# A transformer block with routed experts on one core: full-height bias planes, expert numbers read earlier, joins moved

## The reference

```python
# x: 2 x 1024 x 256, float32; 16 heads of 128 in 4 groups; 8 experts, 2 per token
mod = silu(c) @ wmod                      # sa, ca, ga, sb, cb, gb for each batch
h = layernorm(x) * (1 + ca) + sa
x = x + ga * attention(h, wq, bq, wkv, bkv, wo)   # causal
h = layernorm(x) * (1 + cb) + sb
gate_logits = h @ gate_w.T
top_vals, top_idx = top_k(gate_logits, 2)
w = softmax(top_vals)
y_all = einsum('td,eod->teo', h, expert_w) + expert_b
y_sel = take_along_axis(y_all, top_idx)
x = x + gb * sum(y_sel * w)
```

## Time and profile before

| | |
|---|---|
| timed runs | median 933.34 us of 3 (931.67 to 953.36) |
| profiled execution | 924.07 us, its span 922.3 us |
| mean granted TensorE clock | 0.99 of full |
| busy: PE, VectorE, ScalarE, GpSimd | 888.7 (96%), 741.4 (80%), 544.0 (59%), 325.8 (35%) us |
| chain that ended last | PE 91%, VectorE 5%, ScalarE 2%, issue 1%, DMA 1% |
| DMA | 43.09 MB, mean 47 GB/s |

### The profile page before, as it was taken

How to read it: one execution, slowest core, us unless ns; L and a number is a source line. 1 busy time by engine, 2 the same in 40 slices (tenths; PEclk the granted TensorE clock), 3 DMA queues, 4 the chain that set the end, 5 groups by cost and what they waited for, 6 DMA issues and landing times.

```text
span 922.3 us, 16979 instructions
## 1 busy us (share of the span) xinstructions
PE 888.7 (96%) x5399; PEld 774.2 (84%) x5399; DVE 741.4 (80%) x1672; ACT 544.0 (59%) x1255; POOL 325.8 (35%) x404
## 2 busy tenths in 40 slices
PE   6999999999999999999999999999999999999895
PEld 5788888888888898888888989898988888877573
DVE  6777888888888888878888888888889898865454
ACT  4577666666666666664766666666666666635241
POOL 4464122222222222232434444444222245372815
PEclk9999999999999999999999999999999999999898
DMA  6000710000000000300000000000000003513642
GB/s 240 7 12 13 255 32 12 12 11 11 11 15 15 16 11 7 103 6 1 24 12 14 12 13 12 12 12 12 13 12 13 12 24 133 167 52 105 194 147 80
DMA packets 36651, 43.09 MB, mean 47 GB/s; under 512 B 3061, under 2 KB 33815, under 8 KB 36503
## 3 DMA queue, kind: packets, MB, share of 16 engines
q1 hardware_dynamic: 34216, 35.94, 12.0%
q0 software_dynamic: 2304, 6.29, 2.1%
q10 hardware_dynamic: 64, 0.02, 0.0%
HBM read 32.02 MB, written 15.20 MB: 51 GB/s over the span
## 4 chain that ended last, share of the span: by engine, by line
PE 91%; DVE 5%; ACT 2%; issue 1%; DMA 1%; POOL 0%; SPq 0%; DVEq 0%; ACTq 0%
PE ps_t L1048 13%; PE ps_s L937 10%; PE ps_s L941 9%; PE ps_s L938 9%; PE ps_o L929 7%; PE ps_o L933 7%; PE ps_o L930 7%; PE ps_m L937 3%; PE ps_m L941 3%; PE ps_m L938 3%; PE ps_m L929 3%; PE ps_m L933 3%; PE ps_m L930 3%; PE ps_o L1058 1%; PE ps_s L1299 1%
## 5 line engine op out<-in xcount | busy, mean ns | idle before, releaser
L1410 ACT ACTIVATE pt_hi<-ps_t 128x512 fp32r<-128x512 f32 (+2 forms) x320 | 170.9, 534 | 124.6 <-PE ps_t L1048 124.2
L1460 ACT ACTIVATE probs<-ps_s,neg_max 128x128 f32<-128x128 f32 (+7 forms) x256 | 189.9, 742 | 79.5 <-DVE neg_max L1853 76.2
L1862 DVE TENSOR_TENSOR pt_lo<-ps_t,pt_hi 128x512 fp32r<-128x512 f32 (+2 forms) x320 | 192.2, 601 | 12.9 <-ACT pt_hi L1410 9.0
L1853 DVE TENSOR_REDUCE neg_max<-ps_s 128x1 f32<-128x128 f32 (+7 forms) x256 | 192.3, 751 | 3.7
L1048 PE MATMUL ps_t<-ident,probs 128*128 128x128 f32 x1152 | 188.6, 272 | 0.9 <-DVE pt_lo L1862 0.9
L695 POOL TENSOR_TENSOR q_lo<-raw,q_hi 128x512 fp32r<-128x512 f32 x60 | 77.4, 1289 | 310.8 <-ACT q_hi L1410 310.8
L1048 PEld LDWEIGHTS ps_t<-ident,probs 128*128 128x128 f32 x1152 | 141.9, 141 | 20.7 <-DVE pt_lo L1862 4.9
L937 PE MATMUL ps_s<-k_hi,q_hi 128*128 128x512 f32 (+2 forms) x354 | 148.5, 420 | 2.4 <-ACT probs L1460 2.4
L1900 DVE SCALAR_TENSOR_TENSOR acc<-ps_m,rsum,acc 128x256 f32<-128x256 f32 x256 | 111.3, 476 | 17.6 <-PE ps_m L941 17.0
L941 PE MATMUL ps_s<-k_hi,q_lo 128*128 128x512 f32 (+2 forms) x354 | 123.4, 349 | 0.0
L938 PE MATMUL ps_s<-k_lo,q_hi 128*128 128x512 f32 (+2 forms) x354 | 122.6, 346 | 0.0
(11 more groups left out here) (300 smaller groups left out, 1728.3 us busy)
## 6 DMA issues: line engine op xcount, KB each, us to landing
slot_out_dram<-y_slot SPq DMA_DIRECT2D x38, 128.0 KB, 1.7
wq_raw<-in_L_attn_wq_dram SPq DMA_DIRECT2D x32, 128.0 KB, 2.3
wo_raw<-in_L_attn_wo_dram SPq DMA_DIRECT2D x32, 128.0 KB, 2.0
wkv_raw<-in_L_attn_wkv_dram SPq DMA_DIRECT2D x2, 1024.0 KB, 6.5
acc<-in_L_attn_x_dram SPq DMA_DIRECT2D x2, 1024.0 KB, 16.1
we_raw<-in_L_ffn_expert_w_dram SPq DMA_DIRECT2D x1, 2048.0 KB, 8.4
slot_rows<-slot_rows_dram SPq DMA_DIRECT2D x2, 1024.0 KB, 7.6
slot_rows_dram<-in_L_attn_x_dram SPq DMA_DIRECT2D x1, 1920.0 KB, 17.6
```

The costliest lines, as they stand in the source:

```text
L1410: return nc.scalar.activation(dst, src, ACT.Copy, scale=scale)
L1460: nc.scalar.activation(probs[par][:, prob_offset(i):prob_offset(i) + w], ps_s[:, i % 2, col:col + w], ACT.Exp, bias=neg_max[:, par, i:i + ...
L1853: nc.vector.tensor_reduce(neg_max[:, par, i:i + 1], ps_s[:, i % 2, col:col + w], AXIS_X, ALU.max, negate=True).then_inc(max_set, 1)
L1862: nc.vector.tensor_tensor(pt_lo[:, q % PT, lo:CH], ps_t[:, q % 2, lo:CH], pt_hi[:, q % PT, lo:CH].bitcast(F32), ALU.subtract).then_inc(pt_ ...
```

## The change

- `bias_planes` is cleared on all 128 partitions and `bias_ones` is 128 x 128; both bias matmuls contract over 128 rows, 126 of them zero. GpSimd now does the multiply and the subtraction, in two operations, and VectorE's `bias_low` is gone.
- PE loads the 23 numbers after step 1 of the last frame, and the 15 numbers after the first pair of d = 1.
- On VectorE and ScalarE the halves of near slots 23 and 24 come right behind `mix(1)`. Join 0 alone stays behind `mix(1)`; joins 1 to 5 stand at near slots 2, 4, 7, 9 and 12; joins 6 and 7 inside `mix(2)`, 8 and 9 inside `mix(3)`, 10 and 11 last.
- `finish` of d = 0, 1 and 3 goes to VectorE; GpSimd keeps d = 2, behind its last gather. The ring of gather semaphores is three long. SP's stores follow the new order.

```diff
-GATHERS = 4
+GATHERS = 3
+JOIN_AT = {2: 1, 4: 2, 7: 3, 9: 4, 12: 5}
-        bias_ones = moe("bias_ones", [FREE, P], F32R)
+        bias_ones = moe("bias_ones", [P, P], F32R)
...
+            store_mixed(0)
+            store_mixed(1)
             store_joined(0)
-            store_mixed(0)
-            store_joined(1)
-            store_mixed(1)
             for s in range(SLOTS1):
                 store_slot(s)
-                if s % 2 == 1 and s // 2 + 2 < NT:
-                    store_joined(s // 2 + 2)
-            store_joined(NT)
-            store_mixed(2)
-            for j in range(NT + 1, JOINS):
+                if s - 1 in JOIN_AT:
+                    store_joined(JOIN_AT[s - 1])
+            for j in range(NT - 2, NT + 2):
                 store_joined(j)
             store_mixed(3)
+            store_joined(NT + 2)
+            store_joined(NT + 3)
+            store_mixed(2)
...
             def bias_tables():
+                flat = bias_planes[0:FREE, :, :].rearrange("p x o -> p (x o)")
                 pool.wait_ge(t_mm, NS * (B * HEADS - 1))
                 pool.iota(bias_sign[:, :], pattern=[[0, 8]], base=0, channel_multiplier=1,
...
+                pool.memset(bias_ones[:, :].bitcast(F32), -1.0).then_inc(bias_set, 1)
+                pool.memset(bias_planes[:, :, :].bitcast(F32), 0.0).then_inc(bias_step, 1)
+                pool.wait_ge(bias_step, 2)
                 pool.wait_ge(bias_in, 16 * FREE)
+                pool.tensor_scalar(flat, bias_raw[:, :], 1.0, 1.0, ALU.mult, ALU.mult).then_inc(bias_step, 1)
+                pool.wait_ge(bias_step, 3)
+                pool.tensor_scalar(flat, flat.bitcast(F32), bias_sign[:, 0:1], 1.0, ALU.mult,
+                                   ALU.mult).then_inc(bias_step, 1)
+                pool.wait_ge(bias_step, 4)
+                pool.tensor_tensor(flat, flat.bitcast(F32), bias_raw[:, :], ALU.subtract).then_inc(bias_set, 1)
...
-            for j in range(NT):
-                gather(j)
-                if j == 2:
-                    finish(0)
-                if j == 5:
-                    finish(1)
-            for j in range(NT, JOINS):
+            for j in range(JOINS):
                 gather(j)
             finish(2)
-            finish(3)
...
+                    if very_last and q == 1:
+                        pe.wait_ge(place_set, 1)
+                        first_e.extend(chosen(slot_expert_u, SLOTS))
...
-                nc.tensor.matmul(bank, bias_ones[:, :], bias_planes[0:FREE, bass.ds(e, 1), :].rearrange("p x o -> p (x o)"),
+                nc.tensor.matmul(bank, bias_ones[:, :], bias_planes[:, bass.ds(e, 1), :].rearrange("p x o -> p (x o)"),
...
-            pe.wait_ge(place_set, 1)
-            slot_e = chosen(slot_expert_u, SLOTS)
...
                 for e2 in range(EXPERTS // 2):
                     experts(d, e2)
+                    if d == 1 and e2 == 0:
+                        pe.wait_ge(n_place_set, 1)
+                        near_e.extend(chosen(n_expert_u, SLOTS1))
...
                 mix_first(d)
                 if d + 2 < HALF:
                     hidden2_hi(d + 2)
                 if d == 1:
+                    slot_upper(SLOTS)
+                    slot_upper(SLOTS + 1)
                     weigh_first(0)
-                    weigh_first(1)
-                if d == 3:
-                    weigh_first(NT)
-                    weigh_first(NT + 1)
-            weigh_first(NT + 2)
-            weigh_first(NT + 3)
+                if d == 2:
+                    weigh_first(NT - 2)
+                    weigh_first(NT - 1)
+            for j in range(NT, JOINS):
+                weigh_first(j)
...
-                        if q == 10:
-                            bias_low()
...
                 if d == 2:
-                    slot_lower(SLOTS)
-                    slot_lower(SLOTS + 1)
                     for s in range(SLOTS, ALL_SLOTS):
                         if s + 2 < ALL_SLOTS:
                             slot_lower(s + 2)
-                        i = s - SLOTS
-                        if i % 2 == 1 and i // 2 + 2 < NT:
-                            join(i // 2 + 2)
-                mix(d)
+                        if s - SLOTS in JOIN_AT:
+                            join(JOIN_AT[s - SLOTS])
+                mix(d, {2: {3: NT - 2, 5: NT - 1}, 3: {3: NT, 5: NT + 1}}.get(d, {}))
                 if d + 2 < HALF:
                     hidden2_lo(d + 2)
                 if d == 1:
+                    slot_lower(SLOTS)
+                    slot_lower(SLOTS + 1)
+                    finish(1)
                     join(0)
-                    join(1)
-                if d == 3:
-                    join(NT)
-                    join(NT + 1)
+                elif d != 2:
+                    finish(d)
             join(NT + 2)
             join(NT + 3)
```

More of the change, by code:

```diff
@@ L468, in adaln_block @@
         coef_step, coef_set, first_mixed = sem("coef_step"), sem("coef_set"), sem("first_mixed")
-        moe_mm, mixed, ysum_set, yout_set = (
-            sem("moe_mm"), sem("mixed"), sem("ysum_set"), sem("yout_set"))
+        moe_mm, mixed = sem("moe_mm"), sem("mixed")
+        ysum_set, yout_set = [[sem(f"{name}{i}") for i in range(2)] for name in ("ysum_set", "yout_set")]
         out_done = [sem(f"out_done{i}") for i in range(2)]
@@ L1358, in experts @@
                 pair = slice(2 * e2, 2 * e2 + 2)
-                nc.tensor.matmul(bank, bias_ones[:, :], bias_planes[0:FREE, pair, :].rearrange("p x o -> p (x o)"),
+                nc.tensor.matmul(bank, bias_ones[:, :], bias_planes[:, pair, :].rearrange("p x o -> p (x o)"),
                                  start=True, stop=False)
@@ L1365, in experts @@
                 last.then_inc(moe_mm, 1)
-            def chosen(table, count):
-                return nc.values_load_multi_w_load_instructions(
-                    table[0:1, 0:count], engines=[mybir.EngineType.PE], min_val=0, max_val=EXPERTS - 1,
-                    skip_runtime_bounds_check_because="a sum of seven comparisons lies in 0 to 7")[1]
             n = B * HEADS - 1
@@ L2286, in hidden2_lo, with finish, mix @@
                                         ALU.subtract).then_inc(h2_lo_set, 1)
-            def mix(d):
+            def finish(d):
+                par = d % 2
+                if d >= 2:
+                    dve.wait_ge(out_done[par], 16 * (d // 2))
+                dve.wait_ge(mixed, (d + 1) * LATER_MIXES)
+                nc.vector.tensor_tensor(y_sum[:, par, :], y_even[:, par, :], y_odd[:, par, :], ALU.add).then_inc(ysum_set[par], 1)
+                dve.wait_ge(ysum_set[par], 2 * (d // 2) + 1)
+                nc.vector.tensor_tensor(y_sum[:, par, :], y_sum[:, par, :], row_of["gb1"], ALU.mult).then_inc(ysum_set[par], 1)
+                dve.wait_ge(ysum_set[par], 2 * (d // 2) + 2)
+                nc.vector.tensor_tensor(y_out[:, par, :], y_sum[:, par, :], acc[:, NT + HALF + d, :],
+                                        ALU.add).then_inc(yout_set[par], 1)
+            def mix(d, joins):
                 par = d % 2
@@ L2300, in mix @@
                                                    coef[:, d, e:e + 1], y, ALU.mult, ALU.add).then_inc(mixed, 1)
+                    if e in joins:
+                        join(joins[e])
             def join(j):
```

51 lines of the change are left out of this document (20 added, 31 removed).

## The result

The changed kernel takes 922.68 us (median of 4 runs, 921.62 to 924.42) beside 933.3 for the kernel before: ratio 0.9894 [0.9868, 0.9919]. That is 1.1% less, inside the 2% within which the prediction counts two kernels as the same, and 10.7 us of the 23.1 that it had worked out. The profiled execution took 923.59 us, its span is 921.6.

A forecast was written before the change was run, and what follows sets the result against it. PE, busy 96% of the span, was taken as the bound. Terms for start, slots, pairs, handover, near slots and end summed to 23.1 us, taken from the 933.3 median: 910 us, own range 905 to 915, widened to 902 to 920.

The forecast's parts named there:

- rival 4: Gathers: the three-long semaphore ring makes joins wait for landings; at 12 us landings 25 us lost, 935 us; chance 0.05.
- start, to slot 1, loads off: Start of slot phase: number loads and VectorE's `bias_low` gone, 3.0 us saved, less 0.1 for loads in the last frame.
- slots 1 to 12: Slot phase: full height removes the 0.37 us loss around each bias matmul, 4.4 us saved.
- slots 13 to 15: Slot phase: no gain, because PE waits there for ScalarE's `h` and the cycle stays as long.
- handover, loads off: d = 1 to near slots: shorter `slot_lo` wait, half clock still expected; 3.6 us saved, less 0.5 for number loads.
- near slots 25 to 37: Near slots: 13 x 0.37 = 4.8 us saved, less 1.5 for five joins; net 3.3, bounds 2 and 4.8.
- d = 2, 3 and end: Last expert pairs and joins after PE's last matmul: 3.6 us saved in all, bounds 1 and 5.8.
- Full height: All 54 bias matmuls: 128 rows remove 0.37 us lost a slot, 0.40 a pair; 20.5 us, not all on the path.
- rival 1: Bias matmuls: the height does nothing; only start, handover and end gain, 7 us, giving 926 us; chance 0.08.
- GpSimd's tables: Bias tables before slot 0: multiplication taken at 5.7 us, done at 806.9, just ahead of need, costing nothing.
- Rival 2: Bias tables come late: multiplication at 9.8 us, PE waits 3.8 and stays at half clock; 916 us; chance 0.13.
- Rival 3: Slots: VectorE and ScalarE become the bound, period about 1.25 instead of 1.06; 6.6 us less gain, 917; chance 0.12.

The follow-up runs named there:

- e1: The changed kernel, unaltered, on a chip without the stops: 902.78 us, ratio 0.9718 to the kernel before.
- e15: The changed kernel, unaltered, as control on a chip with the stops: 924.87 us, ratio 0.9919 to the kernel before.
- e17: The changed kernel with batch 0's gathers replaced by plain SyncE loads of the same bytes, on a chip with the stops: 913.05 us.
- e18: The kernel before, unaltered, on a chip with the stops: 943.72 us (1 run).
- e0: The kernel before, unaltered, profiled afresh on a chip without the stops: 928.83 us.
- e3: The changed kernel with both bias matmuls contracting over 2 rows again, on a chip without the stops: 920.83 us, ratio 0.9938 to before.
- e8: The kernel before, unaltered, on another chip without the stops: 927.15 us.
- e12: The kernel before, unaltered, on a third chip without the stops: 936.75 and 943.29 us.
- e2: The kernel before with the full-height bias operands alone, on a chip without the stops: 914.93 us, ratio 0.9839 to before.
- e5: The changed kernel with PE's expert numbers loaded where they were before, on a chip with the stops: 923.68 us.
- e11: The changed kernel with batch 0's gathers replaced by plain SyncE loads, on a chip without the stops: 906.88 us.
- e13: The changed kernel with batch 0's gathers replaced by plain SyncE loads, repeated on another chip without the stops: 906.14 us.

## Why the prediction missed

**The step that failed** is the sentence on the gathers, in rival 4: "the pace is GpSimd's 2.5; beyond, it is (landing + 2.5) / 3". It priced a train of gathers by GpSimd's pace and by landing alone, and the removal of finish(0) and finish(1) from it was costed on VectorE's side only. What the runs showed in its place: on chips A, C and F PE's signals fall behind while the train lasts. In the trace of before, which the sum was made against, nothing shows it, since that record has no stops. The sentence "the saving is the same time on either" failed with it: it holds only where profiled and timed executions pay the same stops. The kernel before took 933.3 on A, 932.9 on C and 932.0 on F; its lowest times there are 930.55 to 931.99, against 923.67 to 925.43 on B, D and E.

Starts of the same matmuls in the record of A against e1 give the size by place: slot 0 is 4.5 us late (811.59, 807.08 for its bias matmul), d = 1 9.3 (859.29, 849.96), near slot 25 20.5 (882.30, 861.83), the last matmul 21.9 (910.54, 888.60), the end 22.5 (921.6, 899.1). So the scatters, which both kernels have, cost the changed one 9.3; the gathers cost 11.2 and, with the half clock behind the stop, some 13. By the times of e15 and e17 the gathers' part is larger: 11.8 us between them, and the plain loads cost 4 elsewhere. What before pays is known less well: 6 us by e18's trace against e0's, 5 to 8 by its lowest times, 9.3 by the distance from its profile to its median, which the prediction carried over. The miss is what the changed kernel pays beyond before, 23.1 - 10.7 = 12.4 us on A, and 910 + 13 = 923 fits it. That the breaks for finish(0) and finish(1) are what kept before out of it is the likely reading, not a shown one.

**The sum itself held** where there are no stops: 23.2 us between the spans 922.3 and 899.1. That it agrees to 0.1 is luck, since two terms are off by 1.8 and 1.5 in opposite directions. Its terms, from starts of bias matmuls in before and in e1:

| term | predicted | measured | from |
|---|---|---|---|
| start, to slot 1, loads off | 2.9 | 3.2 | 812.79, 809.59 |
| slots 1 to 12 | 4.4 | 2.6 | 19.30 to 17.08 up to slot 12, and slot 12 |
| slots 13 to 15 | 0 | 0.0 | 2.11, 2.50, 2.70 against 2.10, 2.50, 2.70 |
| slots 16 to 22 | 2.6 | 2.3 | 10.63, 8.34 |
| eight pairs | 3.2 | 3.3 | 1.70, and four of 0.40 |
| handover, loads off | 3.1 | 4.6 | the rest of 13.25, 8.62 and of 4.77, 3.25 |
| near slots 25 to 37 | 3.3 | 3.7 | 17.99, 14.28 |
| d = 2, 3 and end | 3.6 | 3.6 | 15.82, 12.49; 10.72, 10.50 |

- *Full height* was right, with its size: e3 against e1 gives 15.2, and the prediction's 23.1 less rival 1's 7 is 16. Rival 1 is out. PE's weight loads (PEld) of a bias matmul and of the one behind it, first in the kernel before, then in e1:

```profile
853.69 0.18 PEld L1359 LDWEIGHTS ps_s<-bias_planes,bias_ones 2*128 2x128 f32 x1 [0.36 <-issue]
854.12 0.19 PEld L937 LDWEIGHTS ps_s<-we_hi,h_hi 128*128 128x128 f32 x1 [0.25 <-issue]
...
849.74 0.19 PEld L1369 LDWEIGHTS ps_s<-bias_planes,bias_ones 128*128 128x128 f32 x1
849.97 0.19 PEld L944 LDWEIGHTS ps_s<-we_hi,h_hi 128*128 128x128 f32 x1
```

  The Trainium skill says (TensorE: Matmul & The Clock Gate, LDWEIGHTS) that a weight load's time goes by its columns and the number of rows doesn't matter. The trace agrees: 0.18 us for 2 rows, 0.19 for 128. What the two rows lose is overlap. Their load and the next one start together with their own matmuls (853.69 and 854.12), after 0.36 and 0.25 us without a load. In e1 the bias load starts 0.22 before its matmul of 849.96, and the next one with the bias matmul. So what the Trainium skill says there was no rival to the height: it is about the load's time, not about what the load can overlap.
- *Slots 1 to 12* were over-counted by the prediction's own rule for slots 13 to 15. Slots 3, 5, 7 and 9 last 1.91 us in both kernels: the gate matmuls there wait 0.19 for ScalarE's copy of the turned rows, as slots 13 to 15 do for `h`. Four slots that keep their 0.37, and 0.4 less in slots 1 and 2, are the 1.8 that is missing.
- *Handover*: expected a wait of about 1.5 us with half clock behind. The waits are there, the half clock isn't:

```profile
843.60:858.60 15.00, 13.58 (x65) 11.00 (x63) 8.30 (x24) 3.84 (x10) 11.34 (x13) 1.00 0.70 227
858.60:876.10 17.50, 16.49 (x131) 15.61 (x130) 13.83 (x35) 11.03 (x32) 8.25 (x9) 1.00 0.79 249
```

  (e1, same columns as above.) PE waits 1.42 at 858.37 and 0.91 at 861.63 and goes on at full clock, though 1.39 was followed by half clock in the earlier trace rows. The prediction took the one pause as a rule for the other. It isn't one even for the first: the same pause of 1.39 us was followed by 0.63 in e8 and by 1.00 in e0, e12, e2 and e5.
- *GpSimd's tables*: taken at 5.7 from an operation of 128 columns at 0.36 each; 1.99 was near the lower bound, the copy. Rival 2 is out.
- *Rival 3* didn't come. The near slots take 1.19 each in e1 (875.27 - 858.58 over 14) against 1.07 in the middle of the slot phase, 1.7 us in all, for which the sum had 1.5 (five joins). *Rival 4*, the ring of three, cost 0.31 us once in e1 (0.61 idle at 859.86 where neighbours have 0.30).

## What to carry to other kernels

A two-row matmul between full ones lost 0.4 us here, which filling the rows with zeros won back. A change that sets instructions of one engine closer together, here indirect DMAs, should be priced for what else goes on meanwhile, and not only by that engine's pace. Before a prediction is built on one trace, ask what separates it from the timed runs: 9.3 us lay between the profile and the median here, and no row of that trace explains them. And a wait put down to "issue" or "remote" is late only if the row that it waits for is long done.

## What the runs showed of the hardware

- While GpSimd issues indirect DMAs 1.25 us apart, signals from PE reach ScalarE and VectorE late in the record of the result and on two of the five chips of the experiments: by about 2 us at the end of a train of 8 in the last frame (2.94 idle against 0.86 at the same instruction in e1), by up to 7 in the near scatters, also 8 (slot 21's copy 7.8 us after its last matmul's start against 0.3 in e1), by 11 to 12 with 16. So the length of the train alone doesn't set it. Plain DMAs of the same size do nothing of the kind (e17). Which path is shared, and why chips B, D and E show none of it, no run tells.
- The clock can fall to the 1.2 GHz level behind PE pauses of 0.2 to 0.8 us (slots 13 to 15) and stay there while PE has no pause: for some 24 us in e0, e12 and e18, with two-row matmuls, and for 3.4 us in e11 and e13, with full height. In the first record of the kernel before and in e8, with the same pauses as e0, it doesn't fall there; nor does it in e3, with two rows. Seven traces of full-height kernels on B, D and E have 1.00 from 845 to 852. That two rows leave the array less to do is my reading; no run measured it.
- A weight load of 2 rows takes as long as one of 128 (0.18 and 0.19 us), but in the kernel before neither it nor the load behind it starts ahead of its matmul.
